# Two transformer blocks on one core: the first attention's probabilities transposed by DMA instead of by TensorE

## The chip, the core and the metric

The kernel runs on one core of a Trainium2 chip. A core has TensorE (matrix products, which reads SBUF and writes PSUM), VectorE, ScalarE, GpSimd, and SyncE, which here only issues DMAs. Each engine works through its own stream of instructions in order, and the streams are tied together by semaphores. The metric is the device time of one execution in microseconds (us).

## What is computed

Six sublayers on x of 4 x 256 tokens and 256 features, all in float32:

```
x = x + 0.5 * ffn0(layernorm(x))       # gated, 1024 hidden
x = x + attention0(layernorm(x))       # 16 heads of 128, 4 key/value heads
x = x + 0.5 * ffn0(layernorm(x))
x = x + 0.5 * moe(layernorm(x))        # 8 experts, top 2, and a shared one
x = x + attention1(layernorm(x))       # 16 heads of 16, causal
x = x + 0.5 * moe(layernorm(x))
```

The change touches attention0:

```
q = rope(x @ Wq.T); k = rope(x @ Wk.T); v = x @ Wv.T
scores = einsum('bhqd,bhkd->bhqk', q, k) * 128 ** -0.5
scores = where(iq >= ik - 128, scores, -inf)      # a window, not causal
attn = softmax(scores)
out = einsum('bhqk,bhkd->bhqd', attn, v)
return out.reshape(b, s, 2048) @ Wo.T
```

## The kernel before

**Numbers.** Products with full float32 accuracy are made of float16 halves: every operand is a high half and a low half (`hi = f16(x)`, `lo = f16(x - hi)`), and `product` issues three matmuls, hi x hi, hi x lo and lo x hi (`PASSES`), into one PSUM group. All of them stand under one line, L1492. ScalarE writes the high halves, VectorE or GpSimd the low ones.

**Order.** Every engine has a hand-written stream; nothing is scheduled by a planner. The work runs in two halves `hf` of 512 tokens (two batches each). After the two halves of the first feed-forward (`run_glu(…, 0, 0)` and `(…, 0, 1)`) come `attention0(0, 1, 1)` and `attention0(1, 2, 0)`, then the second feed-forward.

**attention0 of one half.** First come keys, values and the first two queries (`rope_swapped` on ScalarE, L737 and L738, copies the halves of a head crosswise; `rope_cosine` on VectorE, L1244, and `rope_sine` on GpSimd, L590, multiply; `rope_add` on GpSimd, L595, adds; `rope_high` on ScalarE, L742, and `rope_low` on VectorE, L1250, split). Then 32 steps `step0(hf, p, x)`: `p` counts pairs of heads, 0 to 7 (P0 = 8), and `x` 0 to 3 stands for two heads of two batches; a step is one head of one batch, 256 queries by 256 keys. Turns of four steps; a hardware loop runs p = 1 to 6. A step is a software pipeline. On each engine `step0` does, in this order, its part for several items, and `lagged(p, x, k, n)` names the item that entered k steps ago:

- TensorE: scores of the item (into one of two banks), the transposes of the item of 2 steps ago (L1695: four float32 blocks of 128 x 128, by the identity, into a PSUM bank), the value product of the item of 3 steps ago (bank 7), the output projection of the item of 4 steps ago, and at x = 0 and 2 a query projection.
- VectorE: row maximum (L1258) and shift (L1261), a part of the rotation, the low half of the transposed probabilities (L1274), the reciprocal of the row sums (L1278), the low half of the value product (L1281).
- ScalarE: the high half of the transposed probabilities (L751, PSUM to SBUF), two exponentials (L757, each followed by a read of the row sum), the high half of the value product (L763), and at x = 1 and 3 `rope_swapped` for a later query, at x = 0 and 2 `rope_high`.
- GpSimd: `rope_add` at x = 0 and 2, the normalisation (L607: probabilities times the reciprocal, SBUF to SBUF), `rope_sine` at x = 1 and 3.

Probabilities (`PR0`) and their transposed halves (`PT0`) have two buffers each. At the end of the second half the steps (1, P0, 0 to 3), in which only lagged items are left, lie inside the first tile of the second feed-forward on TensorE.

**SyncE's queue.** It loads inputs and weights, then waits for `rows_zero` and `base_set` (both early) and fills two tables of 9216 rows of 258 values in HBM, `XS`, with four stores: for each table one of 9216 rows of 257 zeros from `ROUT` (L469) and one of 9216 single values of 4 bytes from `FREE` (L471). All four count into `dma_z`. The scatter of the expert layer and the first routing wait for that. Next it waits for the end of the attention (`proj_done`) and loads WN and WD.

## Time and profile before

| | |
|---|---|
| median of three runs | 840.13 us (839.39 to 842.07) |
| the profiled execution | 840.43 us, span 838.6 us |
| busy, share of the span | TensorE 85%, VectorE 75%, ScalarE 55%, GpSimd 49% |
| first attention | first scores at 111.5 us, last projection at 355.8 us |

The profile is of one execution. Its span runs from the first to the last instruction; the time is what the device reports for the execution. An engine is busy while an instruction of its own runs; matmuls are pipelined, so that a group of them overlaps the next and their summed times can be more than the time they took. "PE" is TensorE's matmuls, "PEld" its weight loads, "DVE" VectorE, "ACT" ScalarE, "POOL" GpSimd, "SP" SyncE; SPq is SyncE's queue, whose rows show how long an issuing instruction took. Idle time before an instruction stands behind it in brackets with what ended it. "PEclk" is the granted TensorE clock, 1.00 for 2.4 GHz.

### The profile page before, as it was taken

The numbers are of one execution on the slowest core, as the hardware profiler recorded it, in microseconds if no ns is written. First come the engines' busy times: TensorE is split into PE (matmuls) and PEld (weight loads), VectorE is DVE, ScalarE is ACT, GpSimd is POOL, SyncE is SP. The second block draws the span as 40 slices with busy tenths as digits, with TensorE's granted clock in tenths as the row PEclk, the third lists the DMA queues.
The fourth block names the chain that finished last, engine by engine and source line by source line (L and its number), as shares of the span: only waits on it lengthen the run. The fifth ranks groups of instructions, "written<-read, shape, count | busy, mean of one in ns | idle before, by whom it ended". The sixth has DMA issues, their size and how long they took to land. (4 is left out here: it accounts for less than half of the span.)

```text
span 838.6 us, 17601 instructions
## 1 busy us (share of the span) xinstructions
PE 713.9 (85%) x5515; PEld 482.1 (57%) x5515; DVE 627.8 (75%) x1432; ACT 458.0 (55%) x1033; POOL 407.2 (49%) x416
## 2 busy tenths in 40 slices
PE   7898969999979999989898599764797498978985
PEld 3455437777637777755555366433685497545652
DVE  5989878778777778698977577554898596775646
ACT  3444568878757788645423266325574475324541
POOL 4544766667666666358636277324005320351440
PEclk8999989999989999999999799967799598998997
DMA  9999995000000000030001233300000010013324
GB/s 371 329 300 179 214 241 2 0 0 0 2 0 1 0 0 0 1 120 1 1 14 47 81 116 108 132 1 1 1 2 2 13 39 2 2 51 96 115 83 150
DMA packets 64945, 59.07 MB, mean 70 GB/s; under 512 B 29106, under 2 KB 59186, under 8 KB 64370
## 3 DMA queue, kind: packets, MB, share of 16 engines
q1 hardware_dynamic: 60706, 47.85, 23.6%
q0 software_dynamic: 3744, 10.26, 3.4%
q8 instruction: 36, 0.59, 0.3%
q14 instruction: 27, 0.22, 0.1%
q10 hardware_dynamic: 432, 0.15, 0.1%
HBM read 27.92 MB, written 30.33 MB: 69 GB/s over the span
## 5 line engine op out<-in xcount | busy, mean ns | idle before, releaser
L1492 PE MATMUL PS<-XT,WA 128*128 128x512 f16 x432 | 100.3, 380 | 0.0
L607 POOL TENSOR_TENSOR ARENA<-ARENA,ST 128x512 f32<-128x512 f32 x64 | 66.5, 1040 | 66.3 <-DVE ST L1278 66.3
L724 ACT ACTIVATE ARENA<-T 128x512 f16<-128x512 f32 (+1 forms) x56 | 35.2, 628 | 108.5 <-DVE T L1156 101.0
L1492 PE MATMUL PS<-WA,ARENA 128*128 128x256 f16 (+2 forms) x960 | 69.6, 214 | 12.7 <-DVE ARENA L1165 11.7
L1492 PEld LDWEIGHTS PS<-WA,ARENA 128*128 128x128 f16 x960 | 57.2, 97 | 29.5 <-DVE ARENA L1165 17.6
L566 POOL DMA_INDIRECT yt_rows<-WA,DIX x46 | 45.4, 987 | 53.1 <-ACT WA L856 41.5
L1492 PEld LDWEIGHTS PS<-XT,WA 128*128 128x128 f16 (+1 forms) x432 | 42.3, 98 | 44.3 <-issue 1.1
L1258 DVE TENSOR_REDUCE ST<-PS 128x2 f32<-128x512 f32 x64 | 43.9, 686 | 27.9 <-PE PS L1492 27.1
L1492 PE MATMUL PS<-KVR,ARENA 128*128 (+1 forms) x384 | 58.5, 281 | 6.5 <-DVE ARENA L1250 4.2
L757 ACT ACTIVATE ARENA<-PS,ST 128x256 f32<-128x256 f32 x128 | 59.2, 470 | 7.0 <-DVE ST L1261 6.8
L1492 PE MATMUL PS<-XT,WC 128*128 128x512 f16 x264 | 62.2, 386 | 1.0 <-ACT WA L856 1.0
L595 POOL TENSOR_TENSOR T<-T 128x512 f32<-128x512 f32 x40 | 52.6, 1314 | 8.1 <-DVE T L1244 2.6
L590 POOL TENSOR_TENSOR T<-T,ROPE 128x512 f32<-128x512 f32 x40 | 50.9, 1271 | 10.4 <-ACT T L738 10.3
L1492 PE MATMUL PS<-ARENA,KVR 128*128 128x256 f16 x384 | 52.9, 274 | 2.8 <-DVE ARENA L1281 2.5
L1149 DVE SCALAR_TENSOR_TENSOR T<-T,PS 128x512 f32<-128x512 f32 (+1 forms) x56 | 38.0, 679 | 21.8 <-ACT T L716 21.5
L1492 PE MATMUL PS<-XT,WB 128*128 128x512 f16 x192 | 48.3, 390 | 6.1 <-DVE T L1244 4.8
L1492 PE MATMUL PS<-WB,ARENA 128*128 (+1 forms) x384 | 52.4, 273 | 0.3 <-DVE ARENA L1281 0.3
L716 ACT ACTIVATE T<-PS 128x512 f32<-128x512 f32 (+1 forms) x56 | 33.1, 592 | 33.6 <-PE PS L1492 33.5
L1165 DVE TENSOR_TENSOR ARENA<-T,ARENA 128x512 f16<-128x512 f32 (+1 forms) x44 | 40.3, 915 | 13.7 <-ACT ARENA L724 13.2
L541 POOL TENSOR_TENSOR ARENA<-T,ARENA 128x512 f16<-128x512 f32 (+1 forms) x12 | 13.8, 1153 | 73.4 <-ACT ARENA L724 73.4
L1492 PE MATMUL PS<-WE,WA 128*128 x276 | 48.9, 313 | 0.0
L1492 PEld LDWEIGHTS PS<-KVR,ARENA 128*128 128x128 f16 x384 | 33.1, 100 | 25.7 <-issue 6.8
(184 smaller groups left out, 1826.0 us busy)
## 6 DMA issues: line engine op xcount, KB each, us to landing
xs_rows<-ROUT SPq DMA_DIRECT2D x2, 9252.0 KB, 46.9
WA<-xs_rows SPq DMA_DIRECT2D x46, 129.0 KB, 2.0
WB<-wb_dram SPq DMA_DIRECT2D x1, 4096.0 KB, 21.9
WC<-wc_dram SPq DMA_DIRECT2D x1, 2304.0 KB, 27.0
WA<-wa_dram SPq DMA_DIRECT2D x4, 512.0 KB, 7.5
WA<-wa_dram SPq DMA_DIRECT2D x1, 2048.0 KB, 13.2
WA<-yt_rows SPq DMA_DIRECT2D x4, 512.0 KB, 4.0
WB<-yt_rows SPq DMA_DIRECT2D x4, 512.0 KB, 5.8
```

The source lines that it names most:

```text
L541: pl.tensor_tensor(HH[r, a, 1, :], T3[r, :], HH[r, a, 0, :], ALU.subtract).then_inc(hid_lo, 1)
L566: pl.indirect_dma_start(YT, bass.IndirectOffsetOnAxis(ap=DIX[:, b:b + 1], axis=0), YB[:, g % 3, :], None, bounds_check=2 * ROWS + 2 * TOK ...
L590: pl.tensor_tensor(t2, t2, ROPE0[:, 1:2, :].broadcast_to([P, 2, S]), ALU.mult).then_inc(rope_sin, 1)
L595: pl.tensor_tensor(T1[:, a, :], T1[:, a, :], T2[:, a, :], ALU.add).then_inc(rope_sum, 1)
L607: pl.tensor_tensor(pr, pr, rs.broadcast_to([P, 2, S]), ALU.mult).then_inc(norm_done, 1)
L716: sc.activation(T1[r, 0, :], PS[r, GATE[a], :], ACT.Tanh, scale=0.5 / (SX * SW)).then_inc(tanh_done, 1)
L724: sc.activation(HH[r, a, 0, :], T3[r, :], ACT.Copy).then_inc(hid_hi, 1)
L757: sc.activation(PR0[:, x % 2, qt * S:(qt + 1) * S], PS[:, bank, qt * S:(qt + 1) * S], ACT.Exp, bias=ST[:, x % 2, 1, qt:qt + 1], scale=SC0 ...
L1149: v.scalar_tensor_tensor(T2[r, 0, :], T1[r, 0, :], 1.0, PS[r, GATE[a], :], ALU.add, ALU.mult).then_inc(gated, 1)
L1165: v.tensor_tensor(HH[r, a, 1, :], T3[r, :], HH[r, a, 0, :], ALU.subtract).then_inc(hid_lo, 1)
L1258: v.tensor_reduce(ST[:, x % 2, 0, :], PS[:, bank, :].rearrange("p (q k) -> p q k", q=2), AX.X, ALU.max).then_inc(max_done, 1)
L1492: ins = te.matmul(dst, left(a), right(b), start=first and n == 0, stop=last and n == 2, skip_group_check=True)
```

## The change

The probabilities are no longer transposed by TensorE. ScalarE and VectorE split the normalised probabilities in SBUF into float16 halves `PH0`, as soon as GpSimd has normalised them; SyncE issues one transposing DMA for each item, which writes both halves, eight blocks of 128 x 128 float16 (256 KB), from `PH0` to `PT0`; TensorE waits for its semaphore and does the value product one step later than before (4 instead of 3), and the projection 5 instead of 4 steps behind. `PR0`, `PH0` and `PT0` have four buffers each, in memory that is free at that time. The value product goes in turn to banks 6 and 7. With the longer lags the second turn is written out as well (the loop runs p = 2 to 6), and there is one more step at each end.

SyncE has to issue the transpositions, so the four stores that fill the tables are taken out of its stream and put into ScalarE's, between the first feed-forward and `attention0(0, 1, 1)`.

The core of the diff:

```
             if isinstance(i, int) and not 0 <= 4 * i + x - k < 4 * n:
                 return None
-            return (i - 1 if x < k else i), (x - k) % 4
+            return (i - -((x - k) // 4) if x < k else i), (x - k) % 4
...
-            sp.wait_ge(rows_zero, 1)
-            sp.wait_ge(base_set, 5)
-            for table in XS:
-                t3 = table.rearrange("(a p) d -> p a d", p=P)
-                sp.dma_start(t3[:, :, 0:D + 1], ROUT[:, 0:D + 1].rearrange("p (o n) -> p o n", o=1)
-                             .broadcast_to([P, ROWS // P, D + 1])).then_inc(dma_z, 16)
-                sp.dma_start(t3[:, :, D + 1:ROW], FREE[:, :].rearrange("p (a o) -> p a o", o=1),
-                             allow_slow_non_contiguous=True).then_inc(dma_z, 16)
+            def probabilities(hf, p, x):
+                it = NS0 * hf + 4 * p + x
+                sp.wait_ge(ph_lo, it + 1)
+                after(sp, pv_done, it - 3)
+                sp.dma_start(PT0[x].rearrange("p s (g n) -> p (s g) n", n=P), PH0[x].rearrange("p s n -> p (s n)"),
+                             transpose=True).then_inc(pt_in[x], 16)
+
+            for hf in range(2):
+                for p in range(P0):
+                    for x in range(4):
+                        probabilities(hf, p, x)
             sp.wait_ge(proj_done, 2 * NS0)
...
-                pr = PR0[:, x % 2, :].rearrange("p (q k) -> p q k", q=2)
+                pr = PR0[x].rearrange("p (q k) -> p q k", q=2)
...
-                if lagged(p, x, 2, P0):
-                    act.wait_ge(pt_done, st - 1)
-                    after(act, pv_done, st - 3)
-                    bank = odd_bank(hf) + 1 if x % 2 else 6
-                    sc.activation(PT0[:, x % 2, 0, :], PS[:, bank, :], ACT.Copy, scale=SP).then_inc(pt_hi, 1)
+                if item := lagged(p, x, 2, P0):
+                    pp, xx = item
+                    act.wait_ge(norm_done, st - 1)
+                    after(act, pt_in[xx], turned_count(hf, pp - 1))
+                    sc.activation(PH0[xx][:, 0, :], PR0[xx], ACT.Copy, scale=SP).then_inc(ph_hi, 1)
...
             run_glu(act, 0, 1, glu_step, glu_side)
+            act.wait_ge(rows_zero, 1)
+            act.wait_ge(base_set, 5)
+            for xs in XS:
+                t3 = xs.rearrange("(a p) d -> p a d", p=P)
+                act.dma_start(t3[:, :, 0:D + 1], ROUT[:, 0:D + 1].rearrange("p (o n) -> p o n", o=1)
+                              .broadcast_to([P, ROWS // P, D + 1])).then_inc(dma_z, 16)
+                act.dma_start(t3[:, :, D + 1:ROW], FREE[:, :].rearrange("p (a o) -> p a o", o=1),
+                              allow_slow_non_contiguous=True).then_inc(dma_z, 16)
             attention0(0, 1, 1)
...
-                if lagged(p, x, 2, P0):
-                    dve.wait_ge(pt_hi, st - 1)
-                    bank = odd_bank(hf) + 1 if x % 2 else 6
-                    v.scalar_tensor_tensor(PT0[:, x % 2, 1, :], PS[:, bank, :], SP, PT0[:, x % 2, 0, :], ALU.mult,
-                                           ALU.subtract).then_inc(pt_lo, 1)
+                if item := lagged(p, x, 2, P0):
+                    dve.wait_ge(ph_hi, st - 1)
+                    v.scalar_tensor_tensor(PH0[item[1]][:, 1, :], PR0[item[1]], SP, PH0[item[1]][:, 0, :], ALU.mult,
+                                           ALU.subtract).then_inc(ph_lo, 1)
...
-                if lagged(p, x, 2, P0):
-                    pe.wait_ge(norm_done, st - 1)
-                    after(pe, pt_lo, st - 3)
-                    bank = odd_bank(hf) + 1 if a else 6
-                    for qt in range(2):
-                        for kt in range(2):
-                            ins = te.transpose(PS[:, bank, kt * S + qt * P:kt * S + (qt + 1) * P],
-                                               PR0[:, a, qt * S + kt * P:qt * S + (kt + 1) * P], IDF[:, :])
-                    ins.then_inc(pt_done, 1)
-                if item := lagged(p, x, 3, P0):
+                if item := lagged(p, x, 4, P0):
                     pp, xx = item
                     g = pp // (GRP // 2)
-                    pe.wait_ge(pt_lo, st - 2)
-                    after(pe, ot_lo, st - 3)
+                    pe.wait_ge(pt_in[xx], turned_count(hf, pp))
+                    after(pe, ot_lo, st - 5)
+                    pt = PT0[xx].rearrange("p s (q k n) -> p s k q n", q=2, k=2)
                     for kt in range(2):
-                        ins = product(PS[:, OB, 0:S], lambda s: V0[:, s, TPH * hf + 2 * (xx % 2) + kt, ds(g * P, P)],
-                                      lambda s: PT0[:, xx % 2, s, kt * S:(kt + 1) * S], kt == 0, kt == 1)
+                        ins = product(PS[:, OB + a, 0:S].rearrange("p (q n) -> p q n", q=2),
+                                      lambda s: V0[:, s, TPH * hf + 2 * (xx % 2) + kt, ds(g * P, P)],
+                                      lambda s: pt[:, s, kt], kt == 0, kt == 1)
                     ins.then_inc(pv_done, 1)
-                if item := lagged(p, x, 4, P0):
+                if item := lagged(p, x, 5, P0):
                     pp, xx = item
-                    pe.wait_ge(ot_lo, st - 3)
+                    pe.wait_ge(ot_lo, st - 4)
```

## Rows read from the trace of the kernel before

**Rows 1.** The page: engine totals; DMA share in 40 slices (tenths).
```profile
PE 713.9 (85%) x5515; PEld 482.1 (57%) x5515; DVE 627.8 (75%) x1432; ACT 458.0 (55%) x1033; POOL 407.2 (49%) x416
...
DMA  9999995000000000030001233300000010013324
```

**Rows 2.** Windows view, one loop turn: length, busy us by engine, clock, DMA.
```profile
275.69:289.03 13.34, 13.09 (x106) 9.73 (x104) 10.55 (x25) 10.76 (x31) 9.15 (x8) 1.00 0.00 0
```

**Rows 3.** Groups by line in that turn: count, busy us, mean ns, idle before.
```profile
L751 ACT ACTIVATE ARENA<-PS 128x512 f16<-128x512 f32 x4 | 2.4, 597 | 0.5 <-PE PS L1695 0.3
...
L742 ACT ACTIVATE ARENA<-T 128x512 f16<-128x512 f32 x2 | 1.3, 631 | 2.0 <-POOL T L595 2.0
...
L1695 PEld LDWEIGHTS PS<-IDF,ARENA 128*128 128x128 f32 x16 | 1.9, 140 | 0.0
```

**Rows 4.** The timeline of that turn: start us, duration us, engine, line, operation.
```profile
282.85 0.59 ACT L738 ACTIVATE T<-PS 64x512 f32<-64x512 f32 x1
...
283.52 1.28 POOL L590 TENSOR_TENSOR T<-T,ROPE 128x512 f32<-128x512 f32 x1 [0.23 <-ACT T L738]
...
284.31 0.68 DVE L1274 SCALAR_TENSOR_TENSOR ARENA<-PS,ARENA 128x512 f16<-128x512 f32 x1
...
284.94 1.26 POOL L595 TENSOR_TENSOR T<-T 128x512 f32<-128x512 f32 x1
...
286.23 0.63 ACT L742 ACTIVATE ARENA<-T 128x512 f16<-128x512 f32 x1 [0.98 <-POOL T L595]
...
289.59 0.82 PE L1492 MATMUL PS<-ARENA,KVR 128*128 128x256 f16 x6
```

**Rows 5.** The timeline of SyncE's queue (SPq): start us, duration of the issuing instruction.
```profile
41.65 0.44 SPq L469 DMA_DIRECT2D xs_rows<-ROUT  x1
42.13 28.41 SPq L471 DMA_DIRECT2D xs_rows<-FREE  x1
70.58 17.01 SPq L469 DMA_DIRECT2D xs_rows<-ROUT  x1
87.64 28.72 SPq L471 DMA_DIRECT2D xs_rows<-FREE  x1
```

**Rows 6.** Windows while the stores drain; last columns: clock, DMA share, GB/s.
```profile
76.00:80.00 4.00, 4.00 (x27) 2.36 (x25) 2.73 (x4) 2.15 (x4) 1.80 (x3) 1.00 1.88 26
...
108.00:112.00 4.00, 1.25 (x6) 0.40 (x4) 3.98 (x7) 2.48 (x5) 3.85 (x3) 0.51 1.10 334
...
134.00:136.00 2.00, 2.00 (x17) 1.46 (x16) 0.86 (x3) 0.96 (x4) 1.88 (x2) 1.00 0.03 0
```

**Rows 7.** Timeline at the stores' new place, and at the first scores.
```profile
88.62 0.63 ACT L724 ACTIVATE ARENA<-T 128x512 f16<-128x512 f32 x1 [0.81 <-DVE T L1156]
...
90.09 0.59 ACT L737 ACTIVATE T<-PS 64x512 f32<-64x512 f32 x1 [0.83 <-PE PS L1492]
...
93.91 0.59 ACT L737 ACTIVATE T<-PS 64x512 f32<-64x512 f32 x1 [2.62 <-PE PS L1492]
...
111.48 0.34 PEld L1492 LDWEIGHTS PS<-KVR,ARENA 128*128 128x128 f16 x3 [3.50 <-DVE ARENA L1250]
```

**Rows 8.** The timeline of a VectorE operation from SBUF beside GpSimd.
```profile
221.85 1.21 DVE L1250 TENSOR_TENSOR KVR<-T,KVR 128x512 f16<-128x512 f32 x1
...
222.66 1.52 POOL L595 TENSOR_TENSOR T<-T 128x512 f32<-128x512 f32 x1
```

**Rows 9.** The DMA view: issues by line, KB each, median us to landing.
```profile
WE<-wc_dram SPq DMA_DIRECT2D x4, 256.0 KB, 3.7
...
out_dram<-X SPq DMA_DIRECT2D x4, 256.0 KB, 2.1
```

**Rows 10.** The timeline of the attention's end.
```profile
347.13 1.04 POOL L607 TENSOR_TENSOR ARENA<-ARENA,ST 128x512 f32<-128x512 f32 x1 [1.55 <-DVE ST L1278]
...
354.98 0.83 PE L1492 MATMUL PS<-WB,ARENA 128*128 128x256 f16 x6 [0.28 <-DVE ARENA L1281]
```

More of the change, by code:

```diff
@@ L169, in macaron @@
         IDP = sb("IDP", [P, ROWS // P + TT], I32)
+        PR0 = [x[:, o:o + 2 * S] for x, o in ((ARENA, 0), (ARENA, 512), (ROUT, 512), (ROUT, 1024))]
+        PH0, PT0 = ([x[:, o:o + 2 * S].bitcast(F16).rearrange("p (s n) -> p s n", s=2) for x, o in homes]
+                    for homes in (((WA, A_N * JF), (WA, A_N * JF + 512), (WB, B_N * JF), (WB, B_N * JF + 512)),
+                                  ((ARENA, 1024), (ARENA, 1536), (WC, 0), (WE, 0))))
         FREE = sb("FREE", [P, ROWS // P], F32)
@@ L210, in macaron @@
         TXB, GUB, THB, YBK = 0, (4, 5), 1, (6, 7)
-        QB, OB = 4, 7
+        QB, OB = 4, 6
         dma_x = [sem(f"dma_x{i}") for i in range(2)]
@@ L246, in macaron @@
         exp_done, recip_done, norm_done = sem("exp_done"), sem("recip_done"), sem("norm_done")
-        pt_done, pt_hi, pt_lo = sem("pt_done"), sem("pt_hi"), sem("pt_lo")
+        ph_hi, ph_lo = sem("ph_hi"), sem("ph_lo")
+        pt_in = [sem(f"pt_in{i}") for i in range(4)]
         pv_done, ot_hi, ot_lo, proj_done = sem("pv_done"), sem("ot_hi"), sem("ot_lo"), sem("proj_done")
@@ L418, in lagged, with turned_count @@
                 return None
-            return (i - 1 if x < k else i), (x - k) % 4
+            return (i - -((x - k) // 4) if x < k else i), (x - k) % 4
+        def turned_count(hf, p):
+            return 16 * (NS0 // 4 * hf + p + 1)
         P0, P1 = H0 // 2, H1 // 4
@@ L756, in step0 @@
                     for qt in range(2):
-                        sc.activation(PR0[:, x % 2, qt * S:(qt + 1) * S], PS[:, bank, qt * S:(qt + 1) * S],
+                        sc.activation(PR0[x][:, qt * S:(qt + 1) * S], PS[:, bank, qt * S:(qt + 1) * S],
                                       ACT.Exp, bias=ST[:, x % 2, 1, qt:qt + 1], scale=SC0 / SQ ** 2,
                                       accum_out=ST[:, x % 2, 2, qt:qt + 1]).then_inc(exp_done, 1)
-                if lagged(p, x, 3, P0):
-                    act.wait_ge(pv_done, st - 2)
-                    sc.activation(OT0[:, 1 - x % 2, 0, :], PS[:, OB, 0:S], ACT.Copy, scale=1 / SP).then_inc(ot_hi, 1)
+                if lagged(p, x, 4, P0):
+                    act.wait_ge(pv_done, st - 3)
+                    sc.activation(OT0[:, x % 2, 0, :], PS[:, OB + x % 2, 0:S], ACT.Copy, scale=1 / SP).then_inc(ot_hi, 1)
                 if x % 2 and more:
@@ L785, in attention0 @@
                         rope_high(r + i - 1, 1 - i % 2, KT0[:, 0, i - 1, :])
-                    if hf and i < 3:
+                    if hf:
                         step0(0, P0, i)
@@ L803, in attention0 @@
                     step0(hf, 0, x)
-                with act.Fori(1, P0 - 1) as p:
+                for x in range(4):
+                    step0(hf, 1, x)
+                with act.Fori(2, P0 - 1) as p:
                     for x in range(4):
@@ L946, in _ @@
             run_glu(act, 0, 1, glu_step, glu_side)
+            act.wait_ge(rows_zero, 1)
[6 more added lines that the diff above has]
+                              allow_slow_non_contiguous=True).then_inc(dma_z, 16)
             attention0(0, 1, 1)
             attention0(1, 2, 0)
-            for x in range(3):
+            for x in range(4):
                 step0(1, P0, x)
@@ L1278, in step0 @@
                     v.reciprocal(ST[:, x % 2, 3, :], ST[:, x % 2, 2, :]).then_inc(recip_done, 1)
[L1279 to L1281 removed]
+                if lagged(p, x, 4, P0):
+                    dve.wait_ge(ot_hi, st - 3)
+                    v.scalar_tensor_tensor(OT0[:, x % 2, 1, :], PS[:, OB + x % 2, 0:S], 1 / SP, OT0[:, x % 2, 0, :],
                                            ALU.mult, ALU.subtract).then_inc(ot_lo, 1)
@@ L1295, in attention0 @@
                         rope_low(r + i - 1, 1 - i % 2, KT0[:, 1, i - 1, :], KT0[:, 0, i - 1, :])
-                    if hf and i < 3:
+                    if hf:
                         step0(0, P0, i)
@@ L1465, in _ @@
             attention0(1, 2, 0)
-            for x in range(3):
+            for x in range(4):
                 step0(1, P0, x)
@@ L1745, in attention0 @@
                 queries(hf, 0, QB, r + KV0, r + KV0 - 1)
+                if hf:
+                    step0(0, P0 + 1, 0)
                 for i in range(0 if hf else KV0 - 1, TPH - 1):
@@ L1758, in attention0 @@
                     step0(hf, 0, x)
-                with pe.Fori(1, P0 - 1) as p:
+                for x in range(4):
+                    step0(hf, 1, x)
+                with pe.Fori(2, P0 - 1) as p:
                     for x in range(4):
@@ L1927, in last_steps0 @@
                 step0(1, P0, 3)
+                step0(1, P0 + 1, 0)
             def keep_busy(n):
```

5 lines of the change are left out of this document (removed).

## The prediction

> **What bounds the kernel now.** I read the page first: busy times and the slices of the DMA engines [rows 1]. TensorE is busiest over the whole span (713.9 us), and the DMA engines are full in the first six slices of 21 us; but the change lies in the first attention, so that stage decides. In a window of exactly one turn of its loop (four steps, from one normalisation on GpSimd to the same one a turn later, 275.69 to 289.03) TensorE is busy 13.09 of 13.34 us, ScalarE 10.76, VectorE 10.55, GpSimd 9.15 [rows 2]. TensorE sets the turn. The order of time in that turn shows what is close behind: ScalarE copies the swapped query to SBUF (L738, ends 283.44), GpSimd multiplies (L590, from 283.52) and adds (L595, ends 286.20), and only then ScalarE starts L742, having stood idle 0.98 us for GpSimd [rows 4]. That happens twice a turn. It is a wait that TensorE doesn't cause.
>
> The second view is SyncE's queue from 41 us on: four stores that fill the two row tables in HBM are issued one behind the other, and the issuing instructions alone last 0.44, 28.41, 17.01 and 28.72 us [rows 5]. Each waits while the descriptors of the one before it drain: the windows show the engines on them up to about 134 us, at 26 GB/s and a share of 1.88 for the 4-byte pieces of FREE (76 to 80 us), nothing by 134 to 136 [rows 6]. Today they cost nothing: SyncE has nothing else to do, and nobody wants the tables before the first routing, in the second feed-forward.
>
> **The change, part by part.** My sum is made against the profiled execution: span 838.60 us, its time 840.43, so 1.83 lie around the span; the median of the runs is 840.13.
>
> 1. *The table stores move from SyncE to ScalarE's queue*, between the first feed-forward and attention0(0). Four issues move, and everything that stands behind them in ScalarE's order waits: the first is rope_swapped (L737), and behind it all copies, exponentials and halves of the attention. VectorE waits for it (rope_cosine), GpSimd (rope_sine), and through them TensorE, after two K projections. The last ScalarE instruction before them ends at 89.25 (L724, 88.62 + 0.63), the first behind them starts at 90.09 [rows 7], so 0.84 us of idle time is all the cover there is. Price: 0.44 + 28.41 + 17.01 + 28.72 = 74.6, less 0.84 = 73.7 us. From both sides: the engines are no longer busy with weight loads when ScalarE issues them, but the two waits for a ROUT drain are 28.41 with weight loads ahead and 28.72 without, so that other traffic doesn't make them. If the wait of the second ROUT went away, 28.41 + 28.72 = 57.1 would stay; if ScalarE also had to sit out the drain of the last one, 17.0 more, 92. I take 74.6, since the queue issues the same instructions in the same order. During the stall TensorE gets two steps ahead; today ScalarE waits 2.62 us for it at 93.91 [rows 7]. It then starts slowly: after a wait of 2.75 us the granted clock of 108 to 112 us is 0.51, the 1.2 GHz level [rows 6, 7]. So I take 1.4 of the 2.62 back, and nothing more. Its long idle time is inside the 73.7.
>
> 2. *TensorE loses the transposes.* 16 a turn (L1695), and their weight loads of 140 ns are what follows one upon another: 16 x 0.14 = 2.2 us a turn [rows 3]. TensorE would need 13.09 - 2.2 = 10.9.
>
> 3. *What is late next.* ScalarE: 10.76 busy + 2 x 0.98 for GpSimd = 12.7. The wait stays: both ends hang on one another (L738, L590, L595, L742), and what ScalarE does in between doesn't change. The hi copy now reads SBUF: 631 ns, as L742 of the same shape, for 597 (L751): 4 x 0.034 = 0.14 [rows 3]. So 12.9 for 13.34: of the 2.2 us that TensorE loses only 0.4 come out, if nothing else changes.
>
> 4. *The low half on VectorE reads SBUF instead of PSUM.* L1274 takes 0.68 today and lies beside L590 (284.31 against 283.52 to 284.80) [rows 4]. The nearest row with both operands in SBUF beside GpSimd: L1250 at 221.85 took 1.21 us, and the L595 that began beside it took 1.52 for 1.26 [rows 8]. So the low half costs from 0.68, as today, to 1.21, and it lengthens the chain of point 3 by 0 to 0.26, twice a turn, and up to 0.5 if the add must also start later. I take 0.3 each: 12.9 + 0.6 = 13.5, 0.2 longer than today. There are 16 turns: +3 us, bounds -0.45 x 16 = -7 (no collision) and (12.9 + 1.2 - 13.34) x 16 = +12.
>
> 5. *64 transposing DMAs, 256 KB each, on SyncE's queue.* No row shows one. What covers them: the lag grows by one step, and the low half of a step (VectorE, ends 284.99) is wanted by the value product two TensorE steps on (289.59): 4.6 us before anything moves [rows 4]. Beyond that, the loop binds when half, low half, DMA, value product, next scores and exponential exceed the four steps between them: some 6 us of work against 13.4, so that a DMA may take 7.5 us before it costs. Lower bound: a plain DMA of 256 KB to HBM lands in 2.1 us, one of 256 KB from HBM in 3.7 [rows 9]. Upper bound: FREE is 128 x 72 = 9216 pieces of 4 bytes and drains in 17 us, 1.85 ns a piece [rows 5, 6]; a transposition in 1024 rows of 256 bytes would cost 1.9 us at that price, in 65,536 pieces of 4 bytes 121. I take 3 to 4 us, next to the plain ones: hidden, 0. SyncE's wait for ph_lo and pv_done holds up only the next transposition; the loads of WN and WD behind it are issued after the attention as today.
> The Trainium skill bears on this twice. "VectorE: DVE Perf Modes", "The three transpose paths", gives 1309 ns for a 128x128 bf16 block by DMA against 390 by TensorE; eight blocks would then be 10.5 us. "DMA: Bandwidth & Descriptors", "Latency and other measured facts", gives 261 GB/s for a transposing DMA, which is 1.0 us for 256 KB. No run here shows either.
>
> 6. *Ends.* The value product in two banks removes a wait on ot_lo that no row shows as idle: 0. At the end of the second half the last normalisation ends at 348.17 and the last projection at 355.81 [rows 10]; now half 0.63, low half 0.7, DMA 3.5, product 0.8, halves 0.8, projection 0.8 after it: 355.4. But TensorE's other work no longer fills that time so well: +1 at each half's end, +2.
>
> Sum: 840.43 + 73.7 - 1.4 + 3 + 0 + 2 = 917.7, or 918 (9% slower).
>
> **The rivals.**
> *A, as forecast (0.62)*: 918. Its own range goes from 840.4 + 57.1 - 0.8 - 1.4 - 7 = 888 to 840.4 + 92 - 0.8 + 12 + 4 = 948.
> *B1, the transposition is long but pipelined (0.13).* Decides from 7.5 us: each further us costs a fourth in every step, 64 / 4 = 16 us in all. At 9.5 us 950, at 12.5 us 1000. For it: that pieces of 4 bytes cost 17 us for 36 KB. Against it: plain ones of this size.
> *B2, transpositions don't overlap (0.12).* SyncE's queue or the engines become the bound of each step as soon as one takes more than a step, 13.34 / 4 = 3.3 us. By the rows it lies between 1.9 and 121 us; at 5 us a piece 64 x 1.7 = +107, 1025 in all. By the page's 1309 ns per block it would be 64 x (10.5 - 3.3) = +458 and about 1375; as far as the traces bear that out, it is in this case's chance.
> *C, ScalarE's issues hardly block it (0.08).* They cost 4 x 0.44, as the unhindered one [rows 5]. Then the tables drain from 90 to about 182 us beside the first half; the transpositions share the engines with them, and the sum is 840.4 + 1.8 - 0.8 + 3 + 2 = 846, with up to 20 more if a DMA takes 8 to 10 us for the first 20 steps. "Issuing engines are not separate DMA queues" on the skill's DMA page speaks for this one: the time that a sequencer needs to start a DMA is usually small beside the DMA. The trace disagrees for these four: 74.6 us of issue.
> *D, the other side: faster (0.05).* The same mechanism as C, with the tables out of the way and no collision of VectorE and GpSimd: the turn falls to 12.9, 16 x 0.45 = 7 us, 840.4 + 1.0 - 7 = 834 to 840. It needs ScalarE to wait under 7 us in all at the four issues; the rows say 74.6. For it speaks only that no row shows ScalarE issuing a large DMA.
>
> **How the numbers follow.** The likeliest is A, 918. The range takes in A and B1, 0.75, and of B2 the transpositions of 3.3 to 4.5 us (up to 918 + 64 x 1.2 = 995), 0.05: 888 to 1000. Left out are the rest of B2 above, 0.07, and C and D below, 0.13. Faster by over 0.3% (about what a measurement of this kernel can tell from no change): most of D, 0.03. Within 0.3%: 0.03, D and the low end of C. Slower: 0.94.
>
> **What would show it.** Right: four DMA issues on ScalarE's queue from 89 us on, lasting about 0.4, 28, 17 and 28 us, and the first scores at 184 us for 111.48 [rows 7]; TensorE at the 1.2 GHz level after it; the turn 13.0 to 13.6 us with TensorE busy about 10.9 of it and L742 still idle for L595; from the first scores to the end nearly as long as before. The tail after the attention should be unchanged. Wrong: ScalarE issues in a few us (C); TensorE's value products waiting for a DMA in each step (B1, B2); a turn near 11 us, which would mean that the chain over GpSimd gives way with TensorE.

## The result and the profile after

The changed kernel takes 913.12 us (median of 4 runs, 912.82 to 914.44) beside 841.10 us for the kernel before (4 runs): ratio 1.0874, 95% interval 1.0846 to 1.0903. The forecast was 918, range 888 to 1000. The profiled execution has a span of 911.2 us for 838.6, 72.6 us more.

ScalarE's part of the timeline at the stores' new place (start us, duration us, engine, line; ACTq is its issuing side), answering to [rows 5, 7]:

```profile
88.27 0.41 ACTq L964 DMA_DIRECT2D xs_rows<-ROUT  x1
88.71 26.48 ACTq L966 DMA_DIRECT2D xs_rows<-FREE  x1
115.22 17.13 ACTq L964 DMA_DIRECT2D xs_rows<-ROUT  x1
132.38 28.14 ACTq L966 DMA_DIRECT2D xs_rows<-FREE  x1
160.57 0.59 ACT L748 ACTIVATE T<-PS 64x512 f32<-64x512 f32 x1 [71.73 <-issue]
```

Four issues, 72.2 us together, and the copy of the swapped query behind them starts at 160.57, where it started at 90.09 before: +70.5. The windows view (length, busy us by engine, clock, DMA share, GB/s) of that stretch, of its middle, and of one turn of the loop, which answers to [rows 2]:

```profile
88.84:160.57 71.73, 4.87 (x28) 2.44 (x26) 1.78 (x2) 0.00 (x1) 1.23 (x1) 0.56 1.19 242
114.00:132.00 18.00, 0.00 (x0) 0.00 (x0) 0.00 (x0) 0.00 (x0) 0.00 (x0) 0.50 1.53 105
...
232.18:245.52 13.34, 11.41 (x89) 7.99 (x88) 11.25 (x26) 10.71 (x30) 9.67 (x9) 1.00 0.41 79
```

For 71.7 us TensorE is busy 4.87 and the others less than 2; the clock falls to 0.50, the 1.2 GHz level, and the DMA engines alone work. The turn takes 13.34 us, as before, although TensorE is busy 11.41 of it for 13.09. The timeline at four marks shows the total built up: the first scores, the last normalisation of half 0, the first of half 1, the last of half 1.

```profile
180.83 0.35 PEld L1512 LDWEIGHTS PS<-KVR,ARENA 128*128 128x128 f16 x3 [3.03 <-DVE ARENA L1271]
...
287.58 1.04 POOL L618 TENSOR_TENSOR ROUT<-ROUT,ST 128x512 f32<-128x512 f32 x1 [1.55 <-DVE ST L1298]
...
317.39 1.04 POOL L618 TENSOR_TENSOR ARENA<-ARENA,ST 128x512 f32<-128x512 f32 x1 [4.48 <-DVE ST L1298]
...
419.60 1.04 POOL L618 TENSOR_TENSOR ROUT<-ROUT,ST 128x512 f32<-128x512 f32 x1 [1.54 <-DVE ST L1298]
```

Before, the same marks stand at 111.48 [rows 7], 216.10, 244.73 and 347.13 [rows 10]. The two that no row has shown, from the timeline of the kernel before:

```profile
216.10 1.04 POOL L607 TENSOR_TENSOR ARENA<-ARENA,ST 128x512 f32<-128x512 f32 x1 [1.55 <-DVE ST L1278]
...
244.73 1.04 POOL L607 TENSOR_TENSOR ARENA<-ARENA,ST 128x512 f32<-128x512 f32 x1 [4.48 <-DVE ST L1278]
```

So the marks come later by 69.35, 71.48, 72.66 and 72.47 us. The stall gives 70.5, of which 1.1 comes back at once; half 0 adds 2.1, the step to half 1 1.2, half 1 itself nothing (-0.2), the last projection 0.7 (it ends 73.2 later), and behind it 0.6 is won back: 72.6.

The transposing DMAs, from SyncE's queue in the timeline, and the value product that reads one of them:

```profile
238.85 1.23 SPq L477 DMA_TRANSPOSE WC<-WB  x1
...
242.41 0.64 PEld L1512 LDWEIGHTS PS<-WC,KVR 128*128 x6
```

The DMA view (issues, median us to landing) has their groups:

```profile
ARENA<-WA SPq DMA_TRANSPOSE x32, 3.1
...
WC<-WB SPq DMA_TRANSPOSE x16, 3.0
```

An issue takes 1.23 us, a landing 3.0 to 3.1 (medians). Of the one at 238.85 the reader starts 3.56 us after the issue and doesn't wait: 0.5 us is left. At the halves' ends it is not covered: TensorE's multiplications wait for a transposing DMA seven times, 7.0 us together, from 280 to 299 and from 410 to 424 us, the longest here:

```profile
280.34 0.83 PE L1512 MATMUL PS<-ARENA,KVR 128*128 128x256 f16 x6 [2.45 <-DMA ARENA<-WA]
```

Before 280 us and between 299 and 410 it does not wait for one.

### The profile page after: what moved, and what is told of

It reads as the page before. It is cut to its first block and busy times, and to the rows that moved or that the text cites. A ratio compares the mean times of both kernels' runs of the same rounds, so it can differ in the third digit from the quotient of the medians.

```text
span 911.2 us, 17095 instructions
## 1 busy us (share of the span) xinstructions
PE 686.7 (75%) x5259; PEld 452.9 (50%) x5259; DVE 639.1 (70%) x1432; ACT 457.5 (50%) x1033; POOL 415.8 (46%) x416
## 5 line engine op out<-in xcount | busy, mean ns | idle before, releaser
L1512 PE MATMUL PS<-XT,WA 128*128 128x512 f16 x432 | 102.2, 385 | 67.9 <-DVE T L1265 67.9
L1265 DVE TENSOR_TENSOR T<-PS,ROPE 128x512 f32<-128x512 f32 x40 | 27.5, 687 | 75.5 <-ACT T L749 74.7
L1512 PE MATMUL PS<-WA,ARENA 128*128 128x256 f16 (+2 forms) x960 | 68.3, 212 | 12.9 <-DVE ARENA L1186 11.8
L1512 PEld LDWEIGHTS PS<-WA,ARENA 128*128 128x128 f16 x960 | 56.5, 97 | 29.3 <-DVE ARENA L1186 17.7
L606 POOL TENSOR_TENSOR T<-T 128x512 f32<-128x512 f32 x40 | 60.4, 1509 | 8.0 <-DVE T L1265 2.7
L748 ACT ACTIVATE T<-PS 64x512 f32<-64x512 f32 x40 | 23.7, 593 | 77.7 <-issue 71.7
L1512 PEld LDWEIGHTS PS<-KVR,ARENA 128*128 128x128 f16 x384 | 33.6, 101 | 40.3 <-DVE ARENA L1271 12.9
L618 POOL TENSOR_TENSOR ARENA<-ARENA,ST 128x512 f32<-128x512 f32 x32 | 33.2, 1037 | 31.7 <-DVE ST L1298 31.7
L552 POOL TENSOR_TENSOR ARENA<-T,ARENA 128x512 f16<-128x512 f32 (+1 forms) x12 | 13.8, 1154 | 73.3 <-ACT ARENA L735 73.3
## 6 DMA issues: line engine op xcount, KB each, us to landing
WA<-wa_dram SPq DMA_DIRECT2D x1, 2048.0 KB, 12.9
```

Of the source, the lines that this page charges most:

```text
L606: pl.tensor_tensor(T1[:, a, :], T1[:, a, :], T2[:, a, :], ALU.add).then_inc(rope_sum, 1)
L618: pl.tensor_tensor(pr, pr, rs.broadcast_to([P, 2, S]), ALU.mult).then_inc(norm_done, 1)
L748: sc.activation(T2[lo, a, :], PS[hi, bank, :], ACT.Copy).then_inc(rope_swap, 1)
L1265: v.tensor_tensor(T1[:, a, :].rearrange("p (b t) -> p b t", b=2), PS[:, bank, :].rearrange("p (b t) -> p b t", b=2), ROPE0[:, 0:1, :].broa ...
L1512: ins = te.matmul(dst, left(a), right(b), start=first and n == 0, stop=last and n == 2, skip_group_check=True)
```

## The experiments

Every set of runs had the kernel before beside it on its own chip: 847.12 us for the first four below that were timed together (stores_on_act, after_stores_on_sync, after_high_later, before_high_later), 847.54 for no_transposes, low_left_out, two_query_banks and two_query_banks_high_later, 839.65 for loads_between, free_first, best_v and two_transpositions. By the ratio 1.0874 the changed kernel itself would take some 921, 922 and 913 there, which is an estimate. Some expectations below are in microseconds from a kernel before of 840 or 841, so they are compared as ratios. "Turn" is the time from one normalisation to the same one four steps on; where the loop runs steadily it is 13.31 to 13.36 us in the kernel before and 13.34 to 13.38 in the changed one.

### The stall

**stores_on_act**: the kernel before, with nothing changed but the stores' queue.

```diff
-            sp.wait_ge(rows_zero, 1)
-            sp.wait_ge(base_set, 5)
-            for table in XS:
...
+            act.wait_ge(rows_zero, 1)
+            act.wait_ge(base_set, 5)
+            for xs in XS:
```

> The kernel before with one part of the change alone: the four table stores go from SyncE to ScalarE's queue; TensorE still transposes. Theory (ScalarE stands still while the stores are issued): issues of about 0.4, 26, 17 and 28 us on ScalarE's queue, its next instruction 70 us later than before, turn of the loop unchanged at 13.34 us, time 840 + 70 = 910 us (906 to 915). Rival (the stall comes about only together with the transposing DMAs, or a good part of the 72.6 us is paid in the attention): under 880 us.

921.60 us, ratio 1.0857 (1.0826 to 1.0887); the expected 906 to 915 us are 1.079 to 1.089 of 840. The issues last 0.41, 27.95, 17.76 and 29.83, and the copy behind them waits 75.52 us; from first to last normalisation the halves of the attention take 100.1 and 100.2 us, for 100.0 and 102.4 before. This one edit makes the loss; what the rest of the change is worth is within these intervals.

**after_stores_on_sync**: the changed kernel, with the stores back on SyncE, ahead of the transpositions.

> The changed kernel with the four table stores back in SyncE's stream, ahead of the transpositions. Theory: the stall on ScalarE is gone, all else as in the changed kernel: 913 - 70 = 843 us, plus what the first transpositions wait for, since SyncE's rings hold the last FREE store until about 134 us and the first value product is wanted at about 126: 843 to 855, 850 likeliest; the turn stays at 13.35. Rival (the transpositions cost time themselves, hidden by the stall so far): above 860.

871.82 us, ratio 1.0281 (1.0259 to 1.0304). The expected 843 to 855 us are 1.002 to 1.017, so this is some 10 us above their upper end, and on the side of the rival (above 860, 1.022). The trace shows what the rival had not named. SyncE's queue in the timeline, and the row of the waits view (us in all, times, longest) for TensorE's weight loads between 100 and 200 us:

```profile
90.70 31.81 SPq L478 DMA_DIRECT2D xs_rows<-FREE  x1
122.55 19.62 SPq L485 DMA_TRANSPOSE ARENA<-WA  x1
...
143.56 1.34 SPq L485 DMA_TRANSPOSE WC<-WB  x1
```
```profile
PEld PS L1512 <- DMA ARENA<-WA: 19.8, 1, 19.8
```

The first transposition is queued behind the last FREE store, whose 4-byte pieces still have to drain: the windows view has 20 GB/s from 128 to 132 us, then 3 and 2 GB/s until 140. The attention waits 19.8 us for it once. So a transposition is no bystander of the stores: if they share a queue, it pays for them.

**loads_between**: as the last, but the loads of WC and WE stand between the two halves' transpositions instead of ahead of the stores.

```diff
-            sp.dma_start(WC[:, C_N:], wc_in[:, EXP_TILES * C_N:]).then_inc(dma_c, 16)
-            for c, i0, n, e, at in pieces(I_EXP):
...
+                if hf:
+                    break
+                sp.dma_start(WC[:, C_N:], wc_in[:, EXP_TILES * C_N:]).then_inc(dma_c, 16)
+                for c, i0, n, e, at in pieces(I_EXP):
```

> The stores stand on SyncE at their old place, with nothing of the layer's work behind them until the first transposition; the loads of WC and WE, which stood ahead of them, now stand between the two halves' transpositions. If the 19.6 us of the first transposition in after_stores_on_sync were only the rest of the last store (its issue had begun some 32 us before), they go, and the time is that of the kernel before plus what the slower turns and ends give (+2 to +4 us): ratio 1.000 to 1.006. If a transposing DMA pays them by itself whenever it is the queue's first, they stay: ratio about 1.025. If the later loads of WE come too late for their readers, TensorE shows waits for DMA on WE late in the kernel, and the ratio lies between.

844.32 us for 839.65, ratio 1.0060 (1.0037 to 1.0084): the upper end of what the theory gave (1.000 to 1.006). The last FREE store's issue now ends at 98.1 instead of 122.5, and the 19.8 us are gone; the first two transpositions take 1.37 and 1.24 us to issue (their row here merges the two, from 120.56 and 124.43, with the time between them).

```profile
69.10 28.99 SPq L473 DMA_DIRECT2D xs_rows<-FREE  x1
120.56 5.11 SPq L480 DMA_TRANSPOSE ARENA<-WA  x2
```

This is the change without its stall: DMA transpositions in place of TensorE's, with these loads moved, cost this kernel 0.6%. In the trace half 0 takes 104.5 us for 100.0 from its first normalisation to its last, most of it in the first eight steps (29.3 for 25.8), half 1 102.1 for 102.4.

**free_first**: the changed kernel with the four stores in another order.

```diff
-            for xs in XS:
-                t3 = xs.rearrange("(a p) d -> p a d", p=P)
+            tables = [xs.rearrange("(a p) d -> p a d", p=P) for xs in XS]
+            for t3 in tables:
+                act.dma_start(t3[:, :, D + 1:ROW], FREE[:, :].rearrange("p (a o) -> p a o", o=1),
+                              allow_slow_non_contiguous=True).then_inc(dma_z, 16)
+            for t3 in tables:
                 act.dma_start(t3[:, :, 0:D + 1], ROUT[:, 0:D + 1].rearrange("p (o n) -> p o n", o=1)
                               .broadcast_to([P, ROWS // P, D + 1])).then_inc(dma_z, 16)
-                act.dma_start(t3[:, :, D + 1:ROW], FREE[:, :].rearrange("p (a o) -> p a o", o=1),
-                              allow_slow_non_contiguous=True).then_inc(dma_z, 16)
```

> The changed kernel with the four stores on ScalarE in another order: the two FREE stores first, then the two ROUT stores. If an issue lasts as long as the store before it takes to drain, the four issues last about 0.4, 17, 17 and 28 us, 62 us of stall, and the time is about 10 us below the changed kernel's (some 910 on a chip where the kernel before takes 847). If each issue's duration is its own store's cost, they last 17, 17 (or 0.4), 28 and 28 us, and the stall is 73 us or more: same time or longer.

901.09 us in its one run, span 899.3. The timeline and, below it, the issues of each line (duration ns: least, median, most; then the two starts):

```profile
88.10 9.03 ACTq L964 DMA_DIRECT2D xs_rows<-FREE  x2
97.16 43.48 ACTq L967 DMA_DIRECT2D xs_rows<-ROUT  x2
140.69 0.59 ACT L748 ACTIVATE T<-PS 64x512 f32<-64x512 f32 x1 [52.02 <-issue]
```
```profile
L967 ACTq DMA_DIRECT2D xs_rows<-ROUT x2: 13568/21728/29887, 97.2 to 110.8; - x2
```
```profile
L964 ACTq DMA_DIRECT2D xs_rows<-FREE x2: 415/4502/8589, 88.1 to 88.5; - x2
```

The same stores stall ScalarE 52.0 us instead of 71.7. As the first of all, either kind of store took 0.41 us to issue. Behind a FREE store a FREE store took 8.6 and a ROUT store 13.6 (17.1 in the changed kernel); behind a ROUT store a ROUT store took 29.9 and a FREE store 26.5 and 28.1. So the duration belongs to what stands ahead, not to the store. The expected stall of 62 us was too long: 17 and 17 were taken for 8.6 and 13.6, so an issue doesn't wait for exactly the drain that I had put down. Part of what is won is paid back later: the first transposition is issued at 170.82, while the ROUT stores still run (262 GB/s from 170 to 180), and half 0 takes 110.0 us for 102.2, from its first normalisation to its last.

### What sets the turn

The prediction said that TensorE did (13.09 of 13.34 busy), and the chain over GpSimd's add next (12.9 to 13.5).

**no_transposes**: the kernel before, with the 16 transposes of a turn left out and one multiplication by zeros in place of each step's four (so the value product works on zeros).

```diff
-                    for qt in range(2):
-                        for kt in range(2):
-                            ins = te.transpose(PS[:, bank, kt * S + qt * P:kt * S + (qt + 1) * P],
-                                               PR0[:, a, qt * S + kt * P:qt * S + (kt + 1) * P], IDF[:, :])
+                    ins = te.matmul(PS[:, bank, :], ZERO[:, :], ONES[:, :], start=True, stop=True)
```

> The kernel before, with TensorE's four transposes of each step left out: one product of zeros of 512 columns stands in their place, so the probabilities that enter the value product are zero. TensorE has at least 1 us less to do in a turn. Theory of the prediction (TensorE sets the turn at 13.09 of 13.34 us busy): the turn falls to 12.9 us, where ScalarE and its wait for GpSimd take over. New theory (a ring sets it: rope_swapped, cosine, the next query projection into the same PSUM bank, scores, maximum, exponentials, value-product copy, the next rope_swapped, 6.67 us for two steps): the turn stays at 13.3 to 13.35 us.

851.98 us in one run (847.54 before), and the turn is unchanged:

```profile
271.40 1.04 POOL L607 TENSOR_TENSOR ARENA<-ARENA,ST 128x512 f32<-128x512 f32 x1
...
284.74 1.04 POOL L607 TENSOR_TENSOR ARENA<-ARENA,ST 128x512 f32<-128x512 f32 x1
```

13.34 us. TensorE, still shown as busy 12.57 us of it, did not set the turn with its transposes.

**low_left_out**: the changed kernel; VectorE computes the low half for 8 of 512 columns only, the rest of it is zero from the start.

```diff
-                    v.scalar_tensor_tensor(PH0[item[1]][:, 1, :], PR0[item[1]], SP, PH0[item[1]][:, 0, :], ALU.mult,
-                                           ALU.subtract).then_inc(ph_lo, 1)
+                    v.scalar_tensor_tensor(PH0[item[1]][:, 1, 0:8], PR0[item[1]][:, 0:8], SP, PH0[item[1]][:, 0, 0:8],
+                                           ALU.mult, ALU.subtract).then_inc(ph_lo, 1)
```

> The changed kernel, with VectorE's low half of the probabilities cut from 512 to 8 columns (the rest of it zero), so that it doesn't meet GpSimd at the SBUF any more. Theory of the prediction (the chain L749, L601, L606, L753 sets the turn and the meeting lengthens it by 0.3 us twice a turn): L606 falls from 1.53 to 1.27 and the turn from 13.35 to about 12.8. Ring theory (the ring goes through neither L606 nor the low half): L606 falls to 1.27, the turn stays at 13.3 to 13.35.

918.86 us in one run, turn again unchanged (238.36 to 251.68; 13.32 to 13.37 over the loop), though GpSimd's add is back at 1.27 us for 1.53:

```profile
243.90 1.27 POOL L607 TENSOR_TENSOR T<-T 128x512 f32<-128x512 f32 x1
```

So the chain of point 3 of the prediction, over GpSimd's add, is not the bound by itself either. A ring that contains neither a transpose, nor the low half, nor that add could be. It shows in the changed kernel's timeline:

```profile
240.15 0.69 DVE L1279 TENSOR_REDUCE ST<-PS 128x2 f32<-128x512 f32 x1 [0.92 <-PE PS L1512]
...
240.87 0.17 DVE L1282 TENSOR_SCALAR ST<-ST 128x2 f32<-128x2 f32 x1
...
241.07 0.47 ACT L768 ACTIVATE ARENA<-PS,ST 128x256 f32<-128x256 f32 x1
...
241.99 0.38 ACT L774 ACTIVATE ARENA<-PS 128x256 f16<-128x256 f32 x1
...
242.39 0.59 ACT L748 ACTIVATE T<-PS 64x512 f32<-64x512 f32 x1
...
243.01 0.59 ACT L749 ACTIVATE T<-PS 64x512 f32<-64x512 f32 x1
...
243.63 0.69 DVE L1265 TENSOR_TENSOR T<-PS,ROPE 128x512 f32<-128x512 f32 x1
...
244.49 1.47 PE L1512 MATMUL PS<-XT,WB 128*128 128x512 f16 x6 [0.49 <-DVE T L1265]
```

The next query projection writes the one bank QB, and waits (0.49) for the cosine product that still reads it; its six multiplications stand ahead of the next scores; the scores lead to the maximum (0.69), the shift (0.17), the exponentials and the copy (to 242.37), and only behind these ScalarE copies the swapped query, after which comes the cosine. One round serves two steps; the rounds take 6.56 and 6.78 us in turn, 13.34 together. In the kernel before TensorE shows no idle time at that place, but its projection, too, starts 0.16 us after the cosine product has ended (277.61), as it does after the change (0.17, 244.32 to 244.49) and in no_transposes (0.16):

```profile
276.92 0.69 DVE L1244 TENSOR_TENSOR T<-PS,ROPE 128x512 f32<-128x512 f32 x1
...
277.77 1.47 PE L1492 MATMUL PS<-XT,WB 128*128 128x512 f16 x6
```

**two_query_banks**: the changed kernel with a second bank for the queries, one that the change itself had freed.

```diff
+        def query_bank(hf, a):
+            return odd_bank(hf) + 1 if a else QB
...
-                    rope_swapped(r + 2 + x // 2, QB, x // 2)
+                    rope_swapped(r + 2 + x // 2, query_bank(hf, x // 2), x // 2)
...
-                    queries(hf, 2 * p + 2 + x // 2, QB, r + 2 + x // 2, r + 2 + x // 2)
+                    queries(hf, 2 * p + 2 + x // 2, query_bank(hf, x // 2), r + 2 + x // 2, r + 1 + x // 2)
```

> The changed kernel, with the query projections of a turn in two PSUM banks in place of one (the second is the one that held odd transposes), so that a projection no longer waits for the cosine of the one before it. Ring theory: the ring is open, and the next bound is ScalarE with its two waits for L606, 10.7 + 2 x 1.2 = 13.1 us: the turn 12.8 to 13.2, 3 to 8 us faster than the changed kernel. Rival (ring not the bound): turn 13.35, same time.

922.74 us, ratio 1.0883 (1.0842 to 1.0924): as the changed kernel, and a miss. The wait for the cosine is gone, so the ring is open, but the turn is 13.30 to 13.32, against 13.34 to 13.38, and a few hundredths are also what the two halves of one trace differ by. Two rows of the timeline point to what holds it:

```profile
239.38 0.63 ACT L756 ACTIVATE ARENA<-T 128x512 f16<-128x512 f32 x1 [1.22 <-POOL T L609]
...
246.07 0.63 ACT L756 ACTIVATE ARENA<-T 128x512 f16<-128x512 f32 x1 [1.28 <-POOL T L609]
```

ScalarE's 10.66 us of work and these two waits for GpSimd's add are 13.16 of the turn's 13.30; no longer idle time is left on it. So in the changed kernel the chain of the prediction, over GpSimd's add, is as long as the ring within a few hundredths of a microsecond, and both arrive together: the exponentials at 241.07 have had their shift since 241.04, and ScalarE's own conversion of the probabilities ends at 241.13. Shortening the one (low_left_out) or opening the other (two_query_banks) moved nothing. No run does both, so that the two together set the turn is the reading that fits all these runs, and is not shown.

**after_high_later** and **before_high_later**: the changed kernel and the kernel before, with the conversion rope_high (L753, L742) moved from ahead of a step's scores to the next step, just before its exponentials, so that ScalarE no longer stands idle for the add. The same is done at x = 2, for x = 3.

```diff
+                if x == 1 and before:
+                    act.wait_ge(scores, st - 1)
+                    rope_high(r + 1, 1, QT0[:, 1, 0, :])
...
-                if x == 0 and before:
-                    act.wait_ge(scores, st)
-                    rope_high(r + 1, 1, QT0[:, 1, 0, :])
```

> The changed kernel, with ScalarE's rope_high moved from the end of steps x = 0 and 2 to the next step, ahead of its exponentials, so that ScalarE has work while GpSimd multiplies and adds. Theory (ScalarE's wait for L606, 2 x 1.2 us a turn, sets the turn since TensorE no longer does): the turn falls from 13.35 to between 11.5 and 12.5 us, 14 to 16 turns of it, 913 - 20 = 893 us (886 to 902). Rival (the turn is set by the latency of the transposing DMA or by VectorE and GpSimd): the turn stays above 13.1 and the time above 909.

927.16 us, ratio 1.0934 (1.0909 to 1.0959): the turn stays at 13.36. The two halves take 101.8 and 100.5 us, for 102.2 and 102.2 in the changed kernel, so the attention did not grow; the stall is 76.25 us here for 71.73, and 75.52 in stores_on_act, which was timed beside it.

> The same move of rope_high in the kernel before, where TensorE still transposes. Theory (TensorE sets the turn there, 13.09 of 13.34 us): little to win, the turn 13.0 to 13.34, time 835 to 841 us. Rival (ScalarE's wait for GpSimd sets the turn in the kernel before as well): the turn under 12.9, time under 833.

886.92 us, ratio 1.0450 (1.0422 to 1.0479): a turn of 16.6. The move put the conversion between scores and exponentials, that is, into the ring. That alone doesn't explain 3.3 us, since the same move left the changed kernel's turn as it was. Two more things show in this trace, each twice a turn: ScalarE waits 2.1 us for the transposes before it may copy their high half (L751) and convert, and the shift takes 1.1 to 1.3 us for 0.17 beside GpSimd's product, with the exponentials waiting for it:

```profile
151.90 1.27 DVE L1260 TENSOR_SCALAR ST<-ST 128x2 f32<-128x2 f32 x1
...
153.21 0.47 ACT L763 ACTIVATE ARENA<-PS,ST 128x256 f32<-128x256 f32 x1 [0.78 <-DVE ST L1260]
```

What each of them costs was not separated. Both forecasts missed because each rested on one bound read off the traces, an idle time on ScalarE in the one and TensorE's busy time in the other.

**two_query_banks_high_later**: both edits together.

> The changed kernel with both: two query banks, and rope_high in the next step ahead of the exponentials (which alone left the turn at 13.36). Ring theory: with the ring open and ScalarE's wait filled, TensorE (11.4 us busy a turn), VectorE (11.25) and ScalarE (10.7) are what is left: the turn 11.5 to 12.4 us, 15 to 28 us faster than the changed kernel. Rival (the waits of the rotation only move): the turn above 12.8.

921.25 us, ratio 1.0871 (1.0829 to 1.0913), turn 13.22: this is the rival's result. The two waits for the add shrink to 0.70 and 0.76, but another appears, in the timeline:

```profile
244.08 1.04 POOL L621 TENSOR_TENSOR ROUT<-ROUT,ST 128x512 f32<-128x512 f32 x1
...
244.23 0.91 DVE L1284 TENSOR_SCALAR ST<-ST 128x2 f32<-128x2 f32 x1
...
245.17 0.47 ACT L777 ACTIVATE ROUT<-PS,ST 128x256 f32<-128x256 f32 x1 [0.33 <-DVE ST L1284]
```

The shift, two numbers a partition, takes 0.91 us for 0.17 while GpSimd's normalisation runs, and the exponentials wait for it. What holds the turn at 13.22 stays open.

**best_v**: loads_between with the second bank, rope_high behind the exponentials of odd steps and rope_low behind the low half; meant to beat both kernels. The order on ScalarE, behind the exponentials:

```diff
+                if x == 1 and before:
+                    act.wait_ge(scores, st - 1)
+                    rope_high(r + 1, 1, QT0[:, 1, 0, :])
```

> Loads_between and, in the loops, the second query bank, with rope_high after the exponentials of odd steps and rope_low behind the low half, ahead of the reciprocal. By the ring theory the ring of 6.67 us is opened, and ScalarE's work (10.7 us a turn) is next: turn 11.5 to 12.7 instead of 13.34, over 20 turns 13 to 37 us faster than loads_between, ratio to the kernel before 0.96 to 0.99. If ScalarE's waits for the low half only move elsewhere, as they did in two_query_banks_high_later (turn 13.2), the turn stays at 13.1 to 13.4: ratio 0.995 to 1.005.

895.16 us, ratio 1.0650 (1.0613 to 1.0687): the other way. The scores that read the converted query now wait for it:

```profile
202.63 0.50 PE L1516 MATMUL PS<-KVR,ARENA 128*128 x3 [2.37 <-DVE ARENA L1275]
```

Exponentials, conversion, low half, scores and maximum now follow one upon another, and the turn is 16.2 to 18.7 us, mostly 17.3 to 17.5. TensorE's granted clock is 0.80 from 200 to 217.5 us, and six of its multiplications take up to 1.49 us for 0.82; how much of the turn is the order and how much this slower clock was not separated. No order that I tried beat the kernel before.

### What a longer transposition costs

**two_transpositions**: the changed kernel, with a second, unused transposition of the same size ahead of each real one.

```diff
+                after(sp, pad_in, 16 * it)
+                sp.dma_start(PAD0[:, :].rearrange("p (g n) -> p g n", n=P), PH0[x].rearrange("p s n -> p (s n)"),
+                             transpose=True).then_inc(pad_in, 16)
```

> The changed kernel with a second, unused transposition of the same size issued ahead of each real one, into a buffer of its own. By the prediction's margin (7.5 us from a step's exponentials to the value product that reads the transposed halves, 3 us taken by one) two in a row, 1.23 us more of issue and up to 3 us more of landing, stay hidden: the turn stays at 13.34 and the time within 3 us of the changed kernel's (about 920 here). If transposing DMAs share one unit so that two take far more than twice as long, or their traffic slows SBUF accesses of the engines, the turn rises: each microsecond of it is worth 20 in the total, and TensorE's waits for a DMA on WA, WB would show it.

934.59 us in one run, span 932.8: 21.6 more than the changed kernel, not under 3. Landing goes from 3.1 to 3.2 us only, so two don't hinder one another; each real one is just issued 1.3 to 1.5 us later. Most turns take 13.8 to 14.0 us, a few up to 14.8, and TensorE's multiplications wait for a real one 40 times, 34.4 us together, where the changed kernel has 7 waits and 7.0 us:

```profile
249.15 0.83 PE L1517 MATMUL PS<-WE,KVR 128*128 128x256 f16 x6 [0.27 <-DMA WE<-WB]
...
442.68 0.83 PE L1517 MATMUL PS<-WC,KVR 128*128 128x256 f16 x6 [2.11 <-DMA WC<-WB]
```

About 0.5 us in each turn, 5 us in each half (half 0 takes 107.7 for 102.2, half 1 107.0), and the rest at the halves' ends, where nothing covers the DMA: from the last normalisation to the first load behind the attention 17.5 us (432.52 to 450.00) for 9.4 (419.60 to 429.02). The ends measure more than a longer transposition, though: the unused one also waits until the last unused one has landed. In the loop it is issued at most some 0.3 us after its input is ready, but in the last steps of the halves 0.7 to 4.1 us, so that part of the loss there may come from the added order.

## Why the prediction held, point by point

1. *The stall* was sized at 73.7 and measured 70.5, with 57 to 92 as bounds; stores_on_act shows that it explains the result alone, and free_first that the durations in [rows 5] are the queue's backlog. The FREE issues were 1.9 and 0.6 us shorter than on SyncE; the weight loads had ended by then, but no run shows that this is why. The argument that other traffic doesn't make these waits was too strong: in loads_between the first FREE store, issued at 17.99 us beside the input loads, took 35.07 us. The 1.4 for TensorE's head start measured 1.1.
2. *TensorE loses 2.2 us a turn*: 13.09 fell to 11.41, so 1.7. A busy figure holds waiting too, so it can't be reduced by subtraction alone: the same multiplications are 11.41 us busy in a turn of the changed kernel and 11.08 in two_query_banks.
3. *What is late next.* This step failed, in its cause: "TensorE sets the turn" was read off 13.09 of 13.34, and no_transposes shows a turn of 13.34 without the transposes. I followed one chain of the turn [rows 4] and not the second, which waits for a bank. What I took for the next bound, the chain over GpSimd's add, did not move the turn either when it was shortened (low_left_out). The runs put in its place a ring of 13.34 us over the one query bank, in the changed kernel beside the chain over the add, which is as long there. That the forecast of 13.0 to 13.6 held is luck as far as the cause goes: the turn stood at 13.34 before, and the change left it there.
4. *The low half from SBUF* does meet GpSimd: L1294 takes 0.68 or 1.14 to 1.21, L606 1.53 for 1.26, as taken from [rows 8]. Its price of 3 us in the steady turns was not paid, since low_left_out moved none of them. That the halves came out +2.1 and -0.2 is near it by luck: 1.6 of the 2.1 arise in the first six steps of half 0 (20.85 us for 19.27), at a mean clock of 0.90 for 1.00, and in the kernel before the same steps take 19.27 us in half 0 and 21.52 in half 1. The first turn of a half took 12.5 to 12.7 us at a granted clock of 0.94 to 1.00 (half 0 before, both halves of stores_on_act, half 1 of free_first) and 13.9 to 14.9 at 0.70 to 0.88 (half 1 before, both halves after, both of loads_between). Without the low half (low_left_out) the halves take 101.6 and 101.2 us for 102.2 and 102.2, and the step between them 28.6 for 29.8, so that some 3 us may be its cost there; one run doesn't tell it from this.
5. *The transpositions* landed in 3.0 to 3.1 us (taken: 3 to 4) and were hidden in the turn. The threshold was wrong: "7.5 us before it costs" allowed for the whole lag, but the value product reads 3.6 to 4.3 us after the issue, and two_transpositions shows that 1.4 us more cost half a microsecond a turn. The 4.6 us of cover of the same point was the better number. "VectorE: DVE Perf Modes" of the Trainium skill, "The three transpose paths", gives 1309 ns for a 128x128 bf16 block, which for eight blocks is 10.5 us as an estimate; the 3.1 of the trace disagrees, and by the working of B2 that figure stood for about 1375 us. The 261 GB/s of "DMA: Bandwidth & Descriptors" of the Trainium skill, "Latency and other measured facts", give 1.0 us for 256 KB, again as an estimate; from issue to landing the trace has 3.0 to 3.1.
6. *Ends*: +2 taken, 1.2 + 0.7 = 1.9 measured. TensorE's seven waits for a transposing DMA lie in the last turns of the halves and behind them.

Of the rivals, C and D needed ScalarE's issues to be short; they were 72.2 us. B1 and B2 needed a landing of over 7.5 or an occupation of over 3.3 us; TensorE would have begun to wait from about 3.6 us, half a microsecond above what was measured, so the change came far closer to B1 than the prediction said. That the transpositions cost nothing in the turn was right by half a microsecond, not by four.

Open stays what in a queue makes an issue last (how much of the backlog has to be gone), which of the two paths sets the turn, and whether the 0.6% of loads_between can be won back.

## What to carry to other kernels

Before a DMA is moved to another engine's queue, read how long its issue lasts where it stands, not how long it takes to land: a duration that is free where nothing stands behind it is paid in full by everything behind it elsewhere. An engine at 98% busy is not yet the bound; look for the round that closes on itself (here one PSUM bank for every query) and make an experiment that takes the suspected work away. Where it changes nothing, suspect two paths of the same length and take away both. A DMA in a pipeline is hidden up to the moment at which its reader comes for it, which the timeline gives, and not up to the whole lag.

## What the runs showed that I had not expected

- The issue of a transposing DMA behind a store of 4-byte pieces on the same queue lasted 19.6 us for 1.23 (the first of after_stores_on_sync, at 122.55), and TensorE's next weight load waited 19.8 us for it.
- A ROUT store's issue lasted from 0.41 to 29.9 us by what stood ahead of it (free_first and the kernel after).
- A VectorE operation on two numbers a partition took 0.91 us for 0.17 beside a GpSimd operation on 128x512 (two_query_banks_high_later), and 1.27 in before_high_later.
- Two transposing DMAs of 256 KB issued 1.3 us apart landed in 3.2 us each for 3.1: they overlap, and the engines' own operations kept their durations (ScalarE 10.78 us busy in a turn for 10.71).
